# A third Strassen unit from the fifth pass on, factor loads ahead of the transposes, and the next row's halves ahead of the scores

## What is computed

```python
h = maximum(layernorm(x), 0)
q = h @ Wq.T + bq
k = key @ Wk.T + bk
v = value @ Wv.T + bv
scores = (q @ k.T) / 64
a = scores * adj
a = where(abs(a) < 1e-05, -1e9, a)
out = x + (softmax(a) @ v) @ Wm.T + bm
```

## Time and profile before

| | |
|---|---|
| median of 3 runs | 1559.7 us (1559.36 to 1562.26) |
| the profiled execution | 1557.63 us |
| its span | 1555.8 us |
| PE busy | 1517.8 us, 98% |
| DVE busy | 1137.9 us, 73% |
| ACT busy | 649.0 us, 42% |
| POOL busy | 219.3 us, 14% |
| factor loads | 161 of 512 KB, median 4.7 us from issue to landing |
| transposes of probabilities | 252, median 3.4 us |

### The profile page before, as it was taken

One profiled execution on the slowest core, in us unless ns is written; L12 is line 12 of the kernel. 1 busy time (PEld: TensorE's weight loads), 2 busy tenths in 40 slices (PEclk: granted clock), 3 DMA queues, 4 the chain that ended last, 5 costly groups with the idle time before them and its releaser, 6 DMA issues.

```text
span 1555.8 us, 23756 instructions
## 1 busy us (share of the span) xinstructions
PE 1517.8 (98%) x7010; PEld 692.4 (45%) x7010; DVE 1137.9 (73%) x2283; ACT 649.0 (42%) x1076; POOL 219.3 (14%) x285
## 2 busy tenths in 40 slices
PE   8998999999999999999999999999999999999998
PEld 5543444444444444444444444444444444444444
DVE  5989877777777677676767768676776867677672
ACT  5776444434343434344342434434343443434342
POOL 5164000000020102001020200202010020201000
PEclk9999999999999999999999999999999999999999
DMA  9834777667987878898787888878787887778855
GB/s 345 276 79 98 185 200 193 146 142 144 236 203 200 235 187 204 206 203 217 175 204 190 205 207 204 220 173 202 196 210 212 198 221 176 203 195 202 209 136 108
DMA packets 468579, 301.24 MB, mean 194 GB/s; under 512 B 378147, under 2 KB 390691, under 8 KB 468390
## 3 DMA queue, kind: packets, MB, share of 16 engines
q1 hardware_dynamic: 468512, 300.50, 76.5%
q10 hardware_dynamic: 6, 0.01, 0.0%
HBM read 189.54 MB, written 19.40 MB: 134 GB/s over the span
## 4 chain that ended last, share of the span: by engine, by line
PE 78%; DMA 8%; DVE 6%; issue 3%; ACT 3%; SPq 2%; DVEq 0%; ACTq 0%
PE R L874 12%; PE R L876 12%; PE R L875 12%; PE S L874 9%; PE S L876 9%; PE S L875 9%; DMA Kbuf<-key_factors 5%; PE M L874 3%; PE M L876 3%; PE M L875 3%; SPq L611 1%; DMA pT<-osb 1%; DVE Zbuf L1767 1%; PE R L992 1%; DMA pT<-ph 1%
## 5 line engine op out<-in xcount | busy, mean ns | idle before, releaser
L1369 ACT ACTIVATE drop<-Zbuf 128x512 f32<-128x512 f32 x256 | 161.0, 629 | 558.4 <-DVE cmx L1708 302.4
L874 PE MATMUL R<-Vbuf,pT 128*128 128x512 f16 x1008 | 382.1, 379 | 5.8 <-DMA pT<-ph 3.2
L876 PE MATMUL R<-Vbuf,pT 128*128 128x512 f16 x1008 | 382.0, 379 | 0.0
L875 PE MATMUL R<-Vbuf,pT 128*128 128x512 f16 x1008 | 382.0, 379 | 0.0
L874 PE MATMUL S<-Kbuf,qT 128*128 128x512 f16 x650 | 246.4, 379 | 4.3 <-DMA Kbuf<-key_factors 3.8
L875 PE MATMUL S<-Kbuf,qT 128*128 128x512 f16 x650 | 246.3, 379 | 0.0
L876 PE MATMUL S<-Kbuf,qT 128*128 128x512 f16 x650 | 246.3, 379 | 0.0
L1767 DVE SCALAR_TENSOR_TENSOR Zbuf<-S,rs,adjb 128x512 f32<-128x512 f32 x151 | 113.0, 748 | 90.8 <-PE S L876 80.7
L1821 DVE TENSOR_SCALAR drop<-drop,common 128x512 f32<-128x512 f32 x232 | 142.0, 612 | 50.0 <-ACT drop L1369 46.7
L1708 DVE CUSTOM_DVE_ANT_0 Zbuf<-drop,Zbuf 128x512 f32<-128x512 f32 x256 | 177.7, 694 | 0.0
L874 PEld LDWEIGHTS R<-Vbuf,pT 128*128 128x128 f16 x1008 | 98.6, 98 | 127.8 <-DMA pT<-ph 5.9
(11 more groups left out here) (277 smaller groups left out, 2005.2 us busy)
## 6 DMA issues: line engine op xcount, KB each, us to landing
Kbuf<-key_factors SPq DMA_DIRECT2D x161, 512.0 KB, 4.7
adjb<-in_adj_dram SPq DMA_DIRECT2D x256, 256.0 KB, 3.3
xq<-in_x_dram SPq DMA_DIRECT2D x32, 256.0 KB, 2.8
Kbuf<-in_L_gnn_key_dram SPq DMA_DIRECT2D x8, 1024.0 KB, 13.9
xr<-in_x_dram SPq DMA_DIRECT2D x32, 256.0 KB, 2.8
out_dram<-xr SPq DMA_DIRECT2D x31, 256.0 KB, 2.8
Vbuf<-in_L_gnn_value_dram SPq DMA_DIRECT2D x7, 1024.0 KB, 7.7
key_factors<-early SPq DMA_DIRECT2D x48, 128.0 KB, 2.3
```

What stands on the lines that cost most here:

```text
L874: nc.tensor.matmul(ps, lhs[0], rhs[0], start=start, stop=False, skip_group_check=added)
L875: nc.tensor.matmul(ps, lhs[0], rhs[1], start=False, stop=False, skip_group_check=added)
L876: return nc.tensor.matmul(ps, lhs[1], rhs[0], start=False, stop=stop, skip_group_check=added)
L1369: nc.scalar.activation(drop[:, :], tile_of(s.i, s.j), ACT.Abs).then_inc(abs_ready, 1)
```

## The change

- `THREE_FROM` 5 becomes 4: the fifth pass has three units too. `FIRST` 6 becomes 5: the loop begins at the sixth pass.
- The four kept factors of `KEPT_THREE`, which were loaded in steps 10 to 13 of the fifth pass, are loaded in its steps 3 and 4, two each, once all 48 pieces are stored. PE waits for them at unit 2's second step; before, at each unit's first step.
- The start loads of steps 3 to 6 (3 to 5 in a two-unit pass) go to the end of the step before, ahead of the transpose of probabilities and of the adjacency load; each waits for the same scores, (2,B11) in addition for all stored pieces. `AHEAD` stays.
- In step 5 (in the early steps, where `halves_h` falls there) the row's halves move ahead of the step's scores: on VectorE the normalising to the step's beginning, the low half behind the maximum; on ScalarE the high half ahead of the absolute value.

```diff
-        UNIT, NU, MAKE_STEP, FIRST = 4, len(UNITS), 19, 6
-        TWO_FROM, THREE_FROM = 4, 5
+        UNIT, NU, MAKE_STEP, FIRST = 4, len(UNITS), 19, 5
+        TWO_FROM, THREE_FROM = 4, 4
...
-            STARTS_TWO = {3: ((0, "T1"), 5), 4: ((1, "T1"), 4), 5: ((1, "T3"), 6), **AHEAD}
-            STARTS_THREE = {3: ((0, "T1"), 5), 4: ((2, "B11"), 4), 5: ((1, "T1"), 6), 6: ((2, "T1"), 5), **AHEAD}
...
+            AFTER_TWO = {2: ((0, "T1"), 5), 3: ((1, "T1"), 4), 4: ((1, "T3"), 6)}
+            AFTER_THREE = {2: ((0, "T1"), 5), 3: ((2, "B11"), 4), 4: ((1, "T1"), 6), 5: ((2, "T1"), 5)}
...
-                starts = STARTS_THREE if s.three else STARTS_TWO
-                if s.strassen and s.j in starts and (s.prefetch or s.j < 13):
-                    sp.wait_ge(kt_stored, 16 * (2 * len(PIECES) if s.three else 32))
+                if s.strassen and s.j in AHEAD and (s.prefetch or s.j < 13):
                     wait(sp, scores_done, s.t)
-                    load_factor(*starts[s.j])
+                    load_factor(*AHEAD[s.j])
...
+                after = AFTER_THREE if s.three else AFTER_TWO
+                if s.strassen and s.j in after:
+                    what, q = after[s.j]
+                    sp.wait_ge(kt_stored, 16 * (2 * len(PIECES) if what[0] == 2 else 32))
+                    wait(sp, scores_done, s.t + 1)
+                    load_factor(what, q)
                 if s.early:
                     load_probs(s)
...
-                if isinstance(s.t, int) and s.i == THREE_FROM - 1 and 10 <= s.j < 14:
+                if isinstance(s.t, int) and s.i == THREE_FROM and s.j in (3, 4):
                     sp.wait_ge(kt_stored, 16 * 2 * len(PIECES))
-                    sp.wait_ge(kb_stored, 16 * 3 * NU)
-                    sp.wait_ge(scores_done, s.t)
-                    what = list(KEPT_THREE)[s.j - 10]
-                    load_factor(what, KEPT_THREE[what])
+                    for what in list(KEPT_THREE)[2 * (s.j - 3):2 * (s.j - 2)]:
+                        load_factor(what, KEPT_THREE[what])
...
-                        pe.wait_ge(kept_in, 16 * (8 if s.three else 4))
+                        pe.wait_ge(kept_in, 16 * 4)
...
+                        if s.w == 2:
+                            pe.wait_ge(kept_in, 16 * 8)
...
+                if s.early and s.halves_h is not None:
+                    row_high(s)
...
                 if s.early:
+                    if s.halves_h is not None:
+                        normalise(s.halves_h)
                     probs_low(s)
                     tile_max(s)
+                    if s.halves_h is not None:
+                        row_low(s)
...
-                if s.halves_h is not None:
+                if s.halves_h is not None and not s.early:
                     normalise(s.halves_h)
...
+                if s.halves_h is not None and not s.early:
+                    row_low(s)
```

More of the change, by code:

```diff
@@ L1298, in high_of_mixes, with row_high @@
                     .then_inc(s_hi, 1)
+            def row_high(s):
+                wait(act, xn_ready, s.halves_h)
+                wait(act, rstd_ready, s.halves_h)
+                wait(act, q_in, 16 * (s.halves_h - 2))
+                wait(act, o_in, 16 * (s.halves_h - 4))
+                nc.scalar.activation(row[:, 0, :], xq[:, :], ACT.Copy, scale=rstd[:, 2:3]).then_inc(h_hi, 1)
             def weights_of(s):
@@ L1666, in query_low, with row_low @@
                 nc.vector.tensor_tensor(row[:, 1, :], xq[:, :], row[:, 0, :], ALU.subtract).then_inc(q_split, 1)
+            def row_low(s):
+                wait(dve, h_hi, s.halves_h)
+                wait(dve, rstd_ready, s.halves_h)
+                nc.vector.scalar_tensor_tensor(out=row[:, 1, :], in0=xq[:, :], scalar=rstd[:, 2:3], in1=row[:, 0, :],
+                                               op0=ALU.mult, op1=ALU.subtract).then_inc(h_split, 1)
             def out_low(s):
```

## The result

| | before | after |
|---|---|---|
| median (4 runs each) | 1559.53 us (1558.46 to 1562.26) | **1540.17 us** (1538.31 to 1540.74) |
| the profiled execution | 1557.63 us | 1540.49 us |
| its span | 1555.8 us | 1538.7 us |
| fifth pass | 92.68 us | 94.95 us |
| sixth pass | 91.08 us | 91.48 us |

What follows compares the result with a forecast made beforehand. TensorE, busy 98% of the span, was taken as the bound, with 19.0 us of stall in ten passes; 0.7 lost less 17.2 gained made -16.5, so 1541.1 profiled, plus 2.1 for the median: 1543.2 us, range 1537 to 1554.5.

Steps and rivals of the forecast that it cites:

- Part 1: Start loads, steps 3 to 6: issued 2.7 us earlier, all factor-load waits go; transposes land in 4.4 us, with 7.5 available.
- Part 2: Halves ahead of step 5's scores: mixing comes at least 1.3 us sooner, its wait goes; if wrong, 2.4 to 3.5 us stay.
- Part 3: Stall left in ten passes: 1.4 us for two second-half transposes, 0.2 a pass for step 4's mixing; gain 17.2 with last pass.
- Part 4: Fifth pass with three units: six matmuls less gain 1.3 us, stall 4.0 in place of 2.0; 0.7 us lost.
- Part 5: Loop beginning at the sixth pass, one pass fewer written out: put at 0 us.
- The limit of some 358 GB/s: One core's HBM traffic: a 512 KB load takes 1.46 us, the fifth pass's burst 5.9; the sum would be 0.7 worse.
- The rival by which the DMA engines limit the first halves: First halves of passes: earlier issue helps only the group's first loads, half of 17.2 us goes; 1554.3 us, chance 0.18.
- The rival in which waits change their names: Steps 4 and 6: a wait on VectorE's mixing takes the place of each load's wait; 1559 us, chance 0.06.

Runs made afterwards that it cites:

- e3: Changed kernel with the start loads back at the start of the next step, behind transpose and adjacency load; 1559.11 us, ratio 0.9996 to the kernel before.
- e7: Changed kernel with start loads and halves both back where they stood, leaving the fifth pass's third unit and the earlier loop start; 1563.16 us, ratio 1.0022 to before.
- e9: Changed kernel with two extra 512 KB DRAM-to-DRAM copies ahead of the transpose in each of steps 2 to 5 of the looped passes (and the fourth); 1580.38 us.
- e1: Changed kernel with two units in the fifth pass, kept loads back in its steps 10 to 13, loop from the seventh pass; 1538.68 us, ratio 0.9864 to before.
- e5: Changed kernel with the fifth pass's (2,B11) load no longer waiting for the stored pieces; 1536.67 us, ratio 0.9852 to the kernel before.
- e4: e5 with the fifth pass's four kept loads spread one each over steps 4, 7, 8 and 9, each waited for by itself; 1537.28 us, ratio 0.9852 to before.
- e6: Changed kernel with the sixth pass written out, so that the loop begins at the seventh; 1538.72 us, ratio 0.9858 to the kernel before.
- e8: Changed kernel with one extra 512 KB DRAM-to-DRAM copy ahead of the transpose in each of steps 2 to 5 of the looped passes (and the fourth); 1541.97 us.
- e2: Changed kernel with the next row's halves behind step 5's scores again; 1547.65 us, ratio 0.9923 to the kernel before.
- e10: Changed kernel with the edits of both e5 and e6; 1537.13 us, ratio 0.9849 to the kernel before.

## Why the prediction was right, and where not

The sum was 16.5 us and the two profiled executions differ by 17.1. The median came 3.0 us below the forecast, since the forecast had added 2.1 us for the distance between the profiled execution and the median, and this time the median was the lower of the two, by 0.3. By stretch the working held less well than its total:

| stretch | forecast | measured |
|---|---|---|
| seventh to fifteenth pass | 14.0 gained (9/10 of 15.6) | 17.9 gained |
| sixth pass | 1.6 gained | 0.4 lost |
| last pass and tail | 1.6 gained | 2.7 gained |
| fifth pass | 0.7 lost | 2.3 lost |
| up to the fifth pass | 0 | 0.8 lost |

That the total is so near is in part luck: 3.9 and 1.1 us more gained than forecast stand against 2.0, 1.6 and 0.8 less. The larger part, that the stall of the looped passes goes, was not luck. Step by step:

- *Part 1, loads ahead of the transposes* (1.4 us of slack for the worst load, transposes covered up to 7.5 us): right, mechanism and size. No load is waited for in nine passes, the transpose behind the first start load lands in 3.9 us (4.4 forecast), e3 and e7 lose the gain without it, and e9 finds the 7.5 us of step 2's transpose.
- *Part 2, halves ahead* (the wait on the mixing goes; 2.4 to 3.5 us if not): the mechanism was right, the price of its failure was mis-sized. Undone it costs 7.5 us, not 3.5. I took the price from what the view of waits showed before, but there a load that came late to TensorE hid the mixing behind it. With the loads on time the wait shows in every pass.
- *Part 3, what is left* (0.2 us a pass for step 4's mixing, 1.4 for two transposes): both terms were nothing in the nine passes. This step failed, on the safe side, by 1.8 and 1.4 us, and made up for most of what follows. In the last pass the stall on a transpose 36 us before the end fell from 1.46 to 0.77 us. It is 1.46 in e1 too, which has the new load order; what made the difference was not looked for.
- *Part 4, the fifth pass* (1.3 gained by six matmuls, stall of 4.0 us in place of 2.0): the gain is right, the stall was 5.6. By the pitch: ScalarE 0.52 (0.5 forecast), mixing 0.73 (0.6), loads 1.83 and 1.65, together 3.5 (2.9), and a transpose late in the pass, at 506.1, 0.85 us, of which nothing was foreseen. Nearly half of the loads' part has one clear cause. The last store was taken to land at 445.7, as 4.3 us behind 441.3; it was issued at 442.04 and landed in 5.5, at 447.5. Here too 240 of its 256 pieces of 512 bytes have started by 445.8 and the last 16 start one behind the other from 446.7 to 447.1, after an instruction packet of 16 KB (444.57 to 445.61); that the packet held them was not tested. I had let it move a transpose, "which costs nothing", and had not followed the kept loads that stand behind it in the same queue. e5 takes the wait away, and 2.0 us of the pass go. What is left of it, 1.9 us, is the burst itself: e4 took it out of steps 4 to 6 and found it again in the second half. (A slip in the upper bound: 1.1 and the whole 5.2 us make 6.3 of stall, not 6.5.)
- *Part 5, the loop* (0): the term was not nothing. The sixth pass is 1.9 us shorter without it (e6); the gain of the whole, 1.5 us by the medians, is within the intervals. The slices of the page showed no loss where the loop began before, but a slice is 39 us wide. The seventh pass of before, its first loop turn, had a wait for a transpose too, 0.8 us in the view. Begun one pass earlier, the disturbance cost 1.6 us on another transpose and 0.3 on a second.
- The limit of some 358 GB/s that I cited for one core's memory traffic, by which the sum would have been 0.7 us worse, did not show as a limit. In the burst the engines moved 402 GB/s over 6 us, as the stretch from 460 to 466 us of the changed kernel shows. That counts a transpose too, but only 378 of the 1013 packets were under 512 bytes, at most 0.2 of the 2.41 MB, so loads alone ran at 370 or more. I had also left out its condition: the page "DMA: Bandwidth & Descriptors" of the Trainium skill (Measured, under Bandwidth) gives about 358 GB/s for a core when both cores of an HBM domain stream, and 425 for one core alone.

```profile
460.00:466.00 6.00, 4.52 (x22) 1.91 (x21) 3.91 (x8) 2.37 (x4) 0.00 (x0) 1.00 1.05 402
```

The rival by which the DMA engines limit the first halves fell: in the looped passes the same traffic runs without a wait, even with four times 512 KB more (e8); twice that was too much (e9). It was true of the fifth pass alone. The rival in which waits change their names fell too, though e2 shows its size with part 1 alone: 0.72 us a pass.

## What to carry to other kernels

When several late arrivals stand one behind the other, the view of waits prices only the one that came last: give the hidden ones the price that they would have on every turn, not the one seen. When a wait is put into an in-order queue that issues DMAs, list all that stands behind it and take the landing time with a margin: the store's was 4.3 us before and 5.5 after. A load that can leave as soon as its slot is free is better issued ahead of a DMA with several microseconds of room; how much room that is can be counted in matmuls, and it held here.

## What was unexpected of the hardware

**A long wait cost twice.** Behind the longer waits for loads TensorE ran at half clock for a while. In e2 it stood 2.6 us in the fifth pass and started again at full pitch; then the granted clock fell. TensorE's start, and the stretch behind it with the next:

```profile
458.40 0.38 PE L876 MATMUL S<-Kbuf,qT 128*128 128x512 f16 x1 [2.63 <-DMA Kbuf<-key_factors]
```

```profile
459.40:462.40 3.00, 3.00 (x8) 1.06 (x7) 1.17 (x2) 0.63 (x1) 0.00 (x0) 0.50 1.11 366
462.40:466.40 4.00, 4.00 (x20) 1.85 (x19) 3.08 (x6) 2.47 (x4) 0.00 (x0) 0.99 1.03 412
```

Clock 0.50 is 1.2 GHz in place of 2.4. Eight matmuls took 0.43 us each in place of 0.216, 1.7 us more on top of the wait. The same followed the stalls of 2.6 and 3.3 us in e3, of 2.7 in e6 and 3.1 in e7; behind those of 1.8 and 1.65 in the changed kernel, and behind one of 2.4 in e9's sixth pass, the clock stayed at 1.00.

**A free pass is exact.** Without stalls a pass takes 89.35 to 89.39 us, eight times in a row or more, in seven different kernels (the changed one, e1, e4, e5, e6, e8, e10). A stall of a tenth of a microsecond is therefore seen in the length of a pass, long before the median of the runs shows it.
